# Projecting the context's keys and values for two batches at once, in a kernel of four transformer layers

## The chip, the cores and the metric

The kernel runs on one core of a Trainium2 chip, as one program. The metric is device time in microseconds (us), from launch to end. TensorE has two clock levels, 1.2 and 2.4 GHz; the profile gives the clock that was granted as a share of the higher one.

## The reference

The input x is 8 batches of 512 tokens of width 256; each batch has a context of 64 rows of width 192. Four layers follow, each on the layer-normed x, each added to x: cross attention (8 heads of 64) on the context; a 16-expert network of which each token uses 4; a second, top-32 cross attention on the same context (4 heads of 32) whose result sets scale and shift around a long convolution, with an MLP behind it; and an 8-expert layer in which each expert picks its 512 best tokens. What the change touches is the start of both attentions:

```
k = (context @ W_k).reshape(b, j, HEADS, DIM_HEAD)      # 64 rows, 512 columns for each batch
v = (context @ W_v).reshape(b, j, HEADS, DIM_HEAD)
...
K = (x_vision @ Wk).reshape(Bb, Gg, H, DH)              # 64 rows, 128 columns
V = x_vision @ Wv                                       # 64 rows, 256 columns
```

## The kernel before

The first three layers run as a software pipeline over the 8 batches in `layers_block`. A hand-written list, `SCHEDULE`, gives every engine the same order of steps (stage, batch, name, part); each engine takes from it the steps it has a function for, waits on semaphores inside them, and never reorders. Stages of three neighbouring batches overlap: ATTEND of batch b+2, MID of batch b+1 and LAST of batch b. A fourth family of steps, KERN, builds the convolution's kernel in the first 240 us. `experts_block` follows with the last layer: it gathers 512 token rows for each of 8 experts with indirect DMAs issued on GpSimd (POOL, line 2087), multiplies, and adds the rows back with others (line 2097), four of each for an expert.

Everything is in float32, and each float32 matmul appears in the trace as two matmul instructions, each with its own weight load. The step `keys` part 0 projects the context in `ctx_first` (96 partitions, two halves of the width): K into PSUM bank KT, V into bank VT, 16 instructions each with the weights stationary and 64 context columns moving. ScalarE (ACT, lines 1500 and 1501) then copies each bank into `ktbd` and `vtbd`, whose off-diagonal blocks GpSimd has zeroed once at the start (line 793). Part 1 multiplies `ktbd` by the query weights (M, into `m0`), part 2 multiplies `vtbd` by the output weights (VO). `attend` makes the scores S from `m0`; VectorE (DVE) takes their maximum (line 1125), ScalarE the exponential, GpSimd scales them (line 859), and TensorE turns the result (PT, line 1681). The step `text` part 0 does the same for the second attention from `ctx_second`: 12 instructions into bank KV1, then copies into `k1bd` and `v1T`. In the order of the list, odd and even batches have the same steps at nearly the same places: `keys` 0 stands just behind `mlp_out` and beside `back`, whose second half (the FO pair for tiles 2 and 3, lines 1891 and 1895) can only start when VectorE has emptied the banks of tiles 0 and 1 in `film_out` (line 1343).

The SP queue loads the contexts, one batch at a time, some batches ahead (`load_ahead`, `load_second`). The first DVE step of KERN waits until GpSimd has made all its constants (`blanks_made`, 20).

Of the kernel before, what the change touches and what calls it, by code (L numbers as in the profile page):

```python
# [23 lines left out]
P = 128  # L24
B, T, D = 8, 512, 256
NT = T // P
DC = D // P
# [417 lines left out]
def layers_block(nc, ctx, S, A, out):  # L445
    with ExitStack() as tmp:
# [45 lines left out]
        lower_half, upper_half = slice(0, J), slice(J, 2 * J)  # L492
        v1T = sb("v1T", [P, DC, J])
        m1 = sb("m1", [P, DC, H1 * J])
# [130 lines left out]
        def _(sp):  # L625
# [5 lines left out]
            def load_ahead(b):  # L631
                sp.wait_ge(*at(b - 1, "filled", "VT"))
                apart(sp)
                sp.dma_start(ctx0[:], ctx_h[b]).then_inc(*tick("ctx0_loaded"))

# [5 lines left out]
            def load_second(b):  # L641
                sp.wait_ge(*at(b - 1, "filled", "KV1"))
                apart(sp)
                sp.dma_start(ctx1[:], ctx_h[b]).then_inc(*tick("ctx1_loaded"))

# [44 lines left out]
            sp.dma_start(ctx0[:], ctx_h[0]).then_inc(*tick("ctx0_loaded"))  # L690
            load("wk", kv_in)
# [16 lines left out]
            load("values", values_in)  # L708
            sp.dma_start(ctx1[:], ctx_h[0]).then_inc(*tick("ctx1_loaded"))
            for name in ("wk1", "wv1", "b_out", "route"):  # L710
# [718 lines left out]
        def _(a):  # L1429
# [122 lines left out]
            def text(b, part):  # L1552
                if part == 0:
                    a.wait_ge(*at(b, "filled", "KV1"))
                    for h in range(H1):
                        lanes = slice(h * DH1, (h + 1) * DH1)
                        nc.scalar.copy(k1bd[lanes, h * J:(h + 1) * J], bank("KV1")[lanes, 0:J])
                    nc.scalar.copy(v1T[:], bank("KV1")[:, J:3 * J].rearrange("p (k j) -> p k j", k=DC)).then_inc(*tick("emptied", "KV1"))
                if part == 1:
# [110 lines left out]
        def _(pe):  # L1670
# [80 lines left out]
            def keys(b, part):  # L1751
                if part == 0:
                    if first(b):
                        pe.wait_ge(kv_in, 32)
                    pe.wait_ge(*at(b, "ctx0_loaded"))
                    for use, w in (("KT", S["wk"]), ("VT", S["wv"])):
                        o = bank(use)
                        product(b, use, parts=[p for c in range(C0) for p in contract(
                            o[:, c * J:(c + 1) * J], [(w[:, k, c * P:(c + 1) * P], ctx0[:, k, :]) for k in range(2)])])
                if part == 1:  # L1760
                    if first(b):
                        pe.wait_ge(wq_centred, 1)
                    pe.wait_ge(*at(b, "emptied", "KT"))
                    for k in range(DC):
                        product(b, "M", k, parts=[p for c in range(C0) for p in contract(
                            bank("M", k)[:, c * P:(c + 1) * P], [(S["wqT"][:, c, k * P:(k + 1) * P], ktbd[:, c, :])])])
                if part == 2:
                    if first(b):
                        pe.wait_ge(wo_in, 32)
                    pe.wait_ge(*at(b, "emptied", "VT"))  # L1770
                    for k in range(2):
                        product(b, "VO", k, parts=[p for c in range(2) for p in contract(
                            bank("VO", k)[:, c * D:(c + 1) * D], [(vtbd[:, 2 * k + c, :], S["wo"][:, 2 * k + c, :])])])

# [77 lines left out]
            def text(b, part):  # L1852
                if part == 0:
                    if first(b):
                        pe.wait_ge(text_in, 64)
                    pe.wait_ge(*at(b, "ctx1_loaded"))
                    o = bank("KV1")
                    product(b, "KV1", parts=contract(o[:, 0:J], [(S["wk1"][:, k, :], ctx1[:, k, :]) for k in range(2)])
                            + [p for c in range(DC) for p in contract(
                                o[:, (c + 1) * J:(c + 2) * J], [(S["wv1"][:, k, c * P:(c + 1) * P], ctx1[:, k, :]) for k in range(2)])])  # L1860
                if part == 1:
                    pe.wait_ge(*at(b, "emptied", "KV1"))
                    product(b, "MM1", parts=[p for k in range(DC) for p in contract(
                        bank("MM1")[:, k * D:(k + 1) * D], [(S["wq1T"][:, k * P:(k + 1) * P], k1bd[:])])])
                if part == 2:
                    if first(b):
                        pe.wait_ge(film_folded, 3)
                    pe.wait_ge(*open_(b, "VF"))
                    for c in range(DC):
                        low_ = nc.tensor.matmul(bank("VF")[lower_half, :], v1T[:, c, :], S["wfilm"][:, c, 0:512], start=(c == 0), stop=(c == DC - 1))  # L1870
                        if c == DC - 1:
                            low_.then_inc(*tick("film_low"))
                        high_ = nc.tensor.matmul(bank("VF")[upper_half, :], v1T[:, c, :], S["wfilm"][:, c, 512:1024], start=(c == 0), stop=(c == DC - 1))
                    high_.then_inc(*tick("filled", "VF"))
# [433 lines left out]
def build(nc, A, out):  # L2308

    with ExitStack() as ctx:  # L2310
# [11 lines left out]
        with ExitStack() as weights:  # L2322
# [26 lines left out]
            wb("xT", [P, DC, T])  # L2349
            wb("ctx_first", [CK, 2, J])  # L2350
            wb("ctx_second", [CK, 2, J])
            wb("mgate", [P, 1])
# [64 lines left out]
```

## Time and profile before

| | |
|---|---|
| median of 3 runs | 1424.18 us (1421.99 to 1427.73) |
| the profiled execution | 1421.83 us, of it 1420.0 us from the first to the last instruction |
| mean granted TensorE clock | 0.924 |
| TensorE busy (matmul) | 1231.5 us (87%), 5325 instructions |
| VectorE busy | 922.0 us (65%) |
| ScalarE busy | 479.5 us (34%) |
| GpSimd busy | 340.1 us (24%) |
| layers | 0 to 1152 us |
| experts | 1152 to 1420 us |

A row of the timeline is: start, duration from the first to the last of merged instructions, engine, line, operation, output and inputs, shape and count, and in brackets how long the engine was idle before and for whom. A share of busy time is a mean over stages with different limits, so the stages have to be read one by one.

### The profile page before, as it was taken

What the parts mean: (1) busy time and instruction counts of PE and PEld (TensorE: products, weight loads), DVE (VectorE), ACT (ScalarE), POOL (GpSimd) and SP (SyncE); (2) the same over time, 40 slices, a digit from 0 to 9 for tenths busy, and PEclk for the clock granted to TensorE, in tenths of its full rate; (3) what the DMA queues carried; (4) which work ended last, traced back from release to release, by engine and by line L of the source; (5) the groups of instructions that cost most, each with busy time, mean ns of one, the idle gap of its engine ahead of it and who ended that gap; (6) DMA issues with size and microseconds to landing.
All of it is one profiled execution on the core that took longest, in us unless ns stands there. A gap on an engine that the chain in (4) does not pass through costs nothing. (4 is left out here: it accounts for less than half of the span.)

```text
span 1420.0 us, 17680 instructions
## 1 busy us (share of the span) xinstructions
PE 1231.5 (87%) x5325; PEld 743.2 (52%) x5325; DVE 922.0 (65%) x3415; ACT 479.5 (34%) x860; POOL 340.1 (24%) x603
## 2 busy tenths in 40 slices
PE   5776967998999899799989979999687439999996
PEld 3543544555466465455546635554364326667764
DVE  6767897778768767777867877797974581111110
ACT  3534431163153326215332531532412422322221
POOL 4223220033023112202212220320203222322331
PEclk9787978999999999999989999999898659999999
DMA  9002003000300300210030030021000135433421
GB/s 289 25 15 61 19 1 76 18 1 17 90 19 1 106 18 1 61 46 18 15 91 18 1 97 25 3 61 38 1 0 1 61 111 165 143 90 90 96 37 18
DMA packets 45353, 72.54 MB, mean 51 GB/s; under 512 B 8549, under 2 KB 27208, under 8 KB 45130
## 3 DMA queue, kind: packets, MB, share of 16 engines
q1 hardware_dynamic: 39114, 62.88, 15.0%
q0 software_dynamic: 6144, 8.52, 3.4%
q8 instruction: 43, 0.70, 0.2%
q14 instruction: 52, 0.43, 0.1%
HBM read 58.27 MB, written 13.07 MB: 50 GB/s over the span
## 5 line engine op out<-in xcount | busy, mean ns | idle before, releaser
L835 POOL TENSOR_SCALAR ve<-mv 128x2 f32<-128x2 f32 x74 | 16.9, 228 | 515.2 <-DVE mv L1103 515.1
L1675 PE MATMUL ps<-x,keys 128*128 128x512 f32 x256 | 124.4, 610 | 1.8 <-DVE hT L1197 1.8
L1840 PE MATMUL ps<-hT,values 128*128 128x512 f32 x256 | 120.0, 598 | 0.0
L2290 PE MATMUL experts_ps<-experts_yT,experts_fc 128*128 128x512 f32 x256 | 113.4, 601 | 1.2 <-ACT experts_yT L2215 1.2
L2302 PE MATMUL experts_ps<-experts_fc,experts_hT 128*128 128x256 f32 x512 | 112.0, 379 | 0.8 <-ACT experts_hT L2227 0.8
L1675 PE MATMUL ps<-zT_second,w 128*128 128x512 f32 x224 | 104.5, 606 | 6.2 <-ACT big L1616 3.9
L2302 PEld LDWEIGHTS experts_ps<-experts_fc,experts_hT 128*128 128x128 f32 x512 | 96.7, 190 | 14.5 <-ACT experts_hT L2227 1.6
L1675 PE MATMUL ps<-w,big 128*128 128x256 f32 x448 | 99.0, 379 | 0.8 <-ACT big L1616 0.8
L2199 DVE SCALAR_TENSOR_TENSOR experts_o<-experts_ps,experts_wh,experts_b2w 128x256 f32<-128x256 f32 x32 | 15.5, 484 | 128.7 <-PE experts_ps L2302 128.7
L2227 ACT ACTIVATE experts_hT<-experts_ps,experts_b 128x512 f32<-128x512 f32 x64 | 44.0, 687 | 156.9 <-PE experts_ps L2290 156.9
L1675 PEld LDWEIGHTS ps<-w,big 128*128 128x128 f32 x448 | 84.1, 190 | 12.5 <-ACT big L1616 1.6
L2097 POOL DMA_INDIRECT out_x<-experts_o,experts_idx x32 | 51.8, 1618 | 156.1 <-DVE experts_o L2199 154.2
L1840 PEld LDWEIGHTS ps<-hT,values 128*128 128x128 f32 x256 | 49.1, 192 | 61.2 <-issue 61.0
L2290 PEld LDWEIGHTS experts_ps<-experts_yT,experts_fc 128*128 128x128 f32 x256 | 48.7, 193 | 60.0 <-issue 59.9
L1675 PEld LDWEIGHTS ps<-x,keys 128*128 128x128 f32 x256 | 47.9, 195 | 56.5 <-issue 50.6
L1235 DVE MATCH_REPLACE8 work<-rest,work 128x64 f32<-128x64 f32 x384 | 76.2, 210 | 0.4
L1675 PEld LDWEIGHTS ps<-zT_second,w 128*128 128x128 f32 x224 | 40.9, 193 | 51.7 <-issue 39.5
L1675 PE MATMUL ps<-m,xT 128*128 128x512 f32 x128 | 64.9, 631 | 0.0
L859 POOL TENSOR_TENSOR e_buf<-e_buf,rs 128x512 f32<-128x512 f32 x32 | 33.3, 1042 | 120.8 <-DVE rs L1122 120.8
L1675 PE MATMUL ps<-hT,vo 128*128 128x512 f32 x128 | 59.2, 617 | 0.7 <-ACT hT L1486 0.7
L1231 DVE MAX8 rest<-work 128x8 f32<-128x64 f32 x384 | 57.5, 212 | 0.0
L841 POOL TENSOR_TENSOR rstd<-ve,power 128x2 f32<-128x2 f32 x74 | 54.3, 734 | 6.2
(445 smaller groups left out, 2448.1 us busy)
## 6 DMA issues: line engine op xcount, KB each, us to landing
gT<-expert_gates SPq DMA_DIRECT2D x32, 512.0 KB, 7.9
experts_fc<-in_fc1T SPq DMA_DIRECT2D x8, 1024.0 KB, 5.1
experts_fc<-in_fc2T SPq DMA_DIRECT2D x8, 1024.0 KB, 8.6
xT<-in_xT SPq DMA_DIRECT2D x8, 512.0 KB, 3.6
x<-in_x SPq DMA_DIRECT2D x8, 512.0 KB, 3.5
expert_table<-tb SPq DMA_DIRECT2D x7, 528.0 KB, 9.9
out_x<-x SPq DMA_DIRECT2D x7, 512.0 KB, 9.2
w<-in_W SPq DMA_DIRECT2D x2, 1024.0 KB, 9.5
```

Of the source, the lines that this page charges most:

```text
L835: nc.gpsimd.tensor_scalar(o, i, c, None, ALU.add).then_inc(*tick(*event))
L841: nc.gpsimd.tensor_tensor(o, i, power[:].unsqueeze(1).to_broadcast(i.shape), ALU.pow).then_inc(*tick(*event))
L859: nc.gpsimd.tensor_tensor(probs, probs, rs[:, t, :].unsqueeze(2).to_broadcast([P, H0, J]), ALU.mult).then_inc(*tick("pr", t))
L1231: nc.vector.max(best[:, h, :], src[:, h, :]).then_inc(*tick("tm8", t, n, h))
L1235: nc.vector.match_replace(work[:, t, h, :], best[:, h, :], src[:, h, :], OUT_OF_RANGE).then_inc(*tick("tmr", t, n, h))
L1675: last = nc.tensor.matmul(o, l, r_, start=start, stop=stop)
L1840: last = nc.tensor.matmul(bank("O2", k), S["values"][:, c, k * P:(k + 1) * P], hT[:, c % RING, :], start=(c == 0), stop=(c == HC - 1))
L2097: g.indirect_dma_start(out_rows, bass.IndirectOffsetOnAxis(ap=idx[:, e, c:c + 1], axis=0), o[e % 2][:, c, :], None, compute_op=ALU.add).th ...
L2199: nc.vector.scalar_tensor_tensor(o[s][:, c, :], o_bank(CC * e + c), wh[s][:, c:c + 1], b2w[s][:, c, :], ALU.mult, ALU.add).then_inc(out_ma ...
L2227: nc.scalar.activation(hT[e % 2][:, m, :], g_bank(m), ACT.Gelu_apprx_tanh, bias=b1[:, e, m:m + 1]).then_inc(hidden_made, 1)
L2290: last = nc.tensor.matmul(g_bank(m), fc1[e % 3][:, k, m * P:(m + 1) * P], yT[e % 2][:, k, :], start=(k == 0), stop=(k == DC - 1))
L2302: last = nc.tensor.matmul(o_bank(at), hT[e % 2][:, m, c * P:(c + 1) * P], fc2[e % 3][:, m, :], start=(m == 0), stop=(m == HC - 1))
```

## The change

At an even batch, the contexts of batches b and b+1 lie side by side in doubled tiles, and each projection moves 128 columns in place of 64 into the same PSUM bank. The copies fill both halves of doubled `ktbd`, `vtbd`, `k1bd` and `v1T`. At an odd batch TensorE and ScalarE only wait and count the semaphores on, and the later products read the half `b % 2`. The SP queue loads two contexts at even batches and none at odd ones; at batch 0 it issues one more load of each kind. The tiles grow by 6.5 KB in each partition; the reserved room for descriptors of dynamic (GpSimd-issued) DMAs shrinks from the default 16384 bytes to 8192.

```diff
             def load_ahead(b):
-                sp.wait_ge(*at(b - 1, "filled", "VT"))
+                if b % 2:
+                    return
+                sp.wait_ge(*at(b - 2, "filled", "VT"))
                 apart(sp)
-                sp.dma_start(ctx0[:], ctx_h[b]).then_inc(*tick("ctx0_loaded"))
+                for of in range(2):
+                    sp.dma_start(ctx0[:, :, of, :], ctx_h[b + of]).then_inc(*tick("ctx0_loaded"))
...
                     for use, dst in (("KT", ktbd), ("VT", vtbd)):
                         a.wait_ge(*at(b, "filled", use))
-                        src = bank(use)[:, 0:C0 * J].rearrange("p (c j) -> p c j", c=C0)
-                        nc.scalar.copy(dst[0:64, :, 0:J], src[0:64])
-                        nc.scalar.copy(dst[64:P, :, J:2 * J], src[64:P]).then_inc(*tick("emptied", use))
+                        if b % 2:
+                            apart(a)
+                            a.sem_inc(*tick("emptied", use))
+                            continue
+                        src = bank(use).rearrange("p (c of j) -> p of c j", c=C0, of=2)
+                        nc.scalar.copy(dst[0:64, :, :, 0:J], src[0:64])
+                        nc.scalar.copy(dst[64:P, :, :, J:2 * J], src[64:P]).then_inc(*tick("emptied", use))
...
-                    pe.wait_ge(*at(b, "ctx0_loaded"))
+                    if b % 2 == 0:
+                        pe.wait_ge(*at(b + 1, "ctx0_loaded"))
                     for use, w in (("KT", S["wk"]), ("VT", S["wv"])):
+                        if b % 2:
+                            pe.wait_ge(*open_(b, use))
+                            apart(pe)
+                            pe.sem_inc(*tick("filled", use))
+                            continue
                         o = bank(use)
                         product(b, use, parts=[p for c in range(C0) for p in contract(
-                            o[:, c * J:(c + 1) * J], [(w[:, k, c * P:(c + 1) * P], ctx0[:, k, :]) for k in range(2)])])
+                            o[:, c * P:(c + 1) * P], [(w[:, k, c * P:(c + 1) * P], ctx0[:, k, :, :].rearrange("p of j -> p (of j)")) for k in range(2)])])
...
-            wb("ktbd", [P, C0, P])
-            wb("vtbd", [P, C0, P])
-            wb("k1bd", [P, H1 * J])
+            wb("ktbd", [P, 2, C0, P])
+            wb("vtbd", [P, 2, C0, P])
+            wb("k1bd", [P, 2, H1 * J])
...
-    nc = bacc.Bacc("TRN2", target_bir_lowering=False, num_devices=1)
+    nc = bacc.Bacc("TRN2", target_bir_lowering=False, num_devices=1, dynamic_dma_scratch_size=8192)
```

The step `text` part 0 is changed in the same way (bank KV1, tiles `ctx_second`, `k1bd`, `v1T`).

## Rows read from the trace of the kernel before

**Rows 1.** Windows: busy us of each engine (instructions), granted clock, DMA share, GB/s.

```profile
150.00:250.00 100.00, 78.72 (x478) 50.98 (x477) 85.50 (x325) 34.52 (x59) 15.75 (x28) 0.86 0.14 34
850.00:950.00 100.00, 98.45 (x377) 56.67 (x375) 79.05 (x344) 31.82 (x57) 17.96 (x34) 0.98 0.11 31
```

**Rows 2.** Timeline of TensorE: K, V, FO pair and M of batch 4.

```profile
516.23 1.90 PE L1675 MATMUL ps<-ctx_first,wk 96*128 96x64 f32 x16
517.96 1.95 PE L1675 MATMUL ps<-ctx_first,wv 96*128 96x64 f32 x16
519.85 0.39 PE L1891 MATMUL ps<-film_bias,ones_bf 64*128 64x512 bf16 x2
521.02 2.05 PE L1675 MATMUL ps<-ktbd,wqT 128*128 128x128 f32 x16
522.91 1.89 PE L1675 MATMUL ps<-wo,vtbd 128*128 128x256 f32 x8
```

**Rows 3.** Timeline of TensorE: KV1 of batch 1, and what follows it.

```profile
246.94 0.56 PE L1675 MATMUL ps<-ctx_second,wk 96*128 96x64 f32 x4
...
248.23 1.94 PE L1675 MATMUL ps<-x,keys 128*128 128x512 f32 x4
```

**Rows 4.** Timeline, batch 1: VectorE's waits for TensorE behind `keys`.

```profile
167.88 0.63 DVE L1231 MAX8 top<-ps 128x8 f32<-128x64 f32 x4 [0.38 <-PE ps L1675]
172.54 0.69 DVE L1125 TENSOR_REDUCE mx<-ps 128x8 f32<-128x512 f32 x1 [0.61 <-PE ps L1675]
176.50 0.69 DVE L1125 TENSOR_REDUCE mx<-ps 128x8 f32<-128x512 f32 x1 [0.39 <-PE ps L1675]
```

**Rows 5.** Timeline, batch 7: from `keys` to the first turned probabilities.

```profile
877.76 2.00 PE L1675 MATMUL ps<-ctx_first,wk 96*128 96x64 f32 x16
...
879.57 0.42 DVE L1343 TENSOR_TENSOR xf<-xf,ps 128x256 f32<-128x256 f32 x1
...
881.57 0.61 PE L1891 MATMUL ps<-film_bias,ones_bf 64*128 64x512 bf16 x2
...
883.91 0.42 DVE L1341 TENSOR_TENSOR xf<-yv,ps 128x256 f32<-128x256 f32 x1 [0.88 <-PE ps L1895]
...
889.84 0.69 DVE L1125 TENSOR_REDUCE mx<-ps 128x8 f32<-128x512 f32 x1 [1.31 <-PE ps L1675]
...
893.05 1.04 POOL L859 TENSOR_TENSOR e_buf<-e_buf,rs 128x512 f32<-128x512 f32 x1 [3.31 <-DVE rs L1122]
...
894.46 0.60 PE L1681 MATMUL ps<-ident,e_buf 128*128 128x128 f32 x4
```

**Rows 6.** Timeline, batch 5: the same chain behind `keys`.

```profile
655.81 0.69 DVE L1125 TENSOR_REDUCE mx<-ps 128x8 f32<-128x512 f32 x1 [2.04 <-PE ps L1675]
...
659.42 1.04 POOL L859 TENSOR_TENSOR e_buf<-e_buf,rs 128x512 f32<-128x512 f32 x1 [10.06 <-DVE rs L1122]
...
661.29 0.60 PE L1681 MATMUL ps<-ident,e_buf 128*128 128x128 f32 x4
```

**Rows 7.** Timeline of TensorE: the wait behind KV1 of batch 7.

```profile
977.64 1.98 PE L1675 MATMUL ps<-x,keys 128*128 128x512 f32 x4 [0.34 <-DVE hT L1197]
```

**Rows 8.** Windows just behind `keys` of batches 2 and 7.

```profile
281.00:285.00 4.00, 4.00 (x19) 2.41 (x18) 2.99 (x12) 1.00 (x3) 1.88 (x4) 0.63 0.12 27
881.60:885.50 3.90, 3.90 (x18) 2.31 (x18) 2.82 (x11) 0.80 (x3) 1.86 (x4) 0.60 0.00 0
```

**Rows 9.** Timeline of the start: one zeroed tile, and VectorE's first instruction.

```profile
3.62 0.53 POOL L793 MEMSET ktbd<- 128x512 f32 x1
...
7.33 0.89 DVE L951 TENSOR_TENSOR zT_second<-big 128x256 f32<-128x256 f32 x2 [7.33 <-POOL work L798]
```

**Rows 10.** The page: one group of costs, and DMA issues with median us to landing.

```profile
L2097 POOL DMA_INDIRECT out_x<-experts_o,experts_idx x32 | 51.8, 1618 | 156.1 <-DVE experts_o L2199 154.2
...
experts_rows<-expert_table,experts_idx POOLq DMA_INDIRECT x32, 4.1
out_x<-experts_o,experts_idx POOLq DMA_INDIRECT x32, 3.8
```

More of the change, by code:

```diff
@@ L492, in layers_block @@
         lower_half, upper_half = slice(0, J), slice(J, 2 * J)
-        v1T = sb("v1T", [P, DC, J])
+        v1T = sb("v1T", [P, 2, DC, J])
         m1 = sb("m1", [P, DC, H1 * J])
@@ L641, in load_second @@
             def load_second(b):
-                sp.wait_ge(*at(b - 1, "filled", "KV1"))
+                if b % 2:
+                    return
+                sp.wait_ge(*at(b - 2, "filled", "KV1"))
                 apart(sp)
-                sp.dma_start(ctx1[:], ctx_h[b]).then_inc(*tick("ctx1_loaded"))
+                for of in range(2):
+                    sp.dma_start(ctx1[:, :, of, :], ctx_h[b + of]).then_inc(*tick("ctx1_loaded"))
             def spread_gates(b):
@@ L689, in _ @@
                     sp.dma_start(dst[rows_, :], src).then_inc(par_in, 16)
-            sp.dma_start(ctx0[:], ctx_h[0]).then_inc(*tick("ctx0_loaded"))
+            for of in range(2):
+                sp.dma_start(ctx0[:, :, of, :], ctx_h[of]).then_inc(*tick("ctx0_loaded"))
             load("wk", kv_in)
@@ L708, in _ @@
             load("values", values_in)
-            sp.dma_start(ctx1[:], ctx_h[0]).then_inc(*tick("ctx1_loaded"))
+            for of in range(2):
+                sp.dma_start(ctx1[:, :, of, :], ctx_h[of]).then_inc(*tick("ctx1_loaded"))
             for name in ("wk1", "wv1", "b_out", "route"):
@@ L1554, in text @@
                     a.wait_ge(*at(b, "filled", "KV1"))
+                    if b % 2:
+                        apart(a)
+                        a.sem_inc(*tick("emptied", "KV1"))
+                        return
                     for h in range(H1):
                         lanes = slice(h * DH1, (h + 1) * DH1)
-                        nc.scalar.copy(k1bd[lanes, h * J:(h + 1) * J], bank("KV1")[lanes, 0:J])
-                    nc.scalar.copy(v1T[:], bank("KV1")[:, J:3 * J].rearrange("p (k j) -> p k j", k=DC)).then_inc(*tick("emptied", "KV1"))
+                        nc.scalar.copy(k1bd[lanes, :, h * J:(h + 1) * J], bank("KV1")[lanes, 0:2 * J].rearrange("p (of j) -> p of j", of=2))
+                    nc.scalar.copy(v1T[:], bank("KV1")[:, 2 * J:6 * J].rearrange("p (k of j) -> p of k j", k=DC, of=2)).then_inc(*tick("emptied", "KV1"))
                 if part == 1:
@@ L1765, in keys @@
                         product(b, "M", k, parts=[p for c in range(C0) for p in contract(
-                            bank("M", k)[:, c * P:(c + 1) * P], [(S["wqT"][:, c, k * P:(k + 1) * P], ktbd[:, c, :])])])
+                            bank("M", k)[:, c * P:(c + 1) * P], [(S["wqT"][:, c, k * P:(k + 1) * P], ktbd[:, b % 2, c, :])])])
                 if part == 2:
@@ L1772, in keys @@
                         product(b, "VO", k, parts=[p for c in range(2) for p in contract(
-                            bank("VO", k)[:, c * D:(c + 1) * D], [(vtbd[:, 2 * k + c, :], S["wo"][:, 2 * k + c, :])])])
+                            bank("VO", k)[:, c * D:(c + 1) * D], [(vtbd[:, b % 2, 2 * k + c, :], S["wo"][:, 2 * k + c, :])])])
             def attend(b, s):
@@ L1855, in text @@
                         pe.wait_ge(text_in, 64)
-                    pe.wait_ge(*at(b, "ctx1_loaded"))
+                    if b % 2:
+                        pe.wait_ge(*open_(b, "KV1"))
+                        apart(pe)
+                        pe.sem_inc(*tick("filled", "KV1"))
+                        return
+                    pe.wait_ge(*at(b + 1, "ctx1_loaded"))
                     o = bank("KV1")
-                    product(b, "KV1", parts=contract(o[:, 0:J], [(S["wk1"][:, k, :], ctx1[:, k, :]) for k in range(2)])
+                    both = [ctx1[:, k, :, :].rearrange("p of j -> p (of j)") for k in range(2)]
+                    product(b, "KV1", parts=contract(o[:, 0:P], [(S["wk1"][:, k, :], both[k]) for k in range(2)])
                             + [p for c in range(DC) for p in contract(
-                                o[:, (c + 1) * J:(c + 2) * J], [(S["wv1"][:, k, c * P:(c + 1) * P], ctx1[:, k, :]) for k in range(2)])])
+                                o[:, (c + 1) * P:(c + 2) * P], [(S["wv1"][:, k, c * P:(c + 1) * P], both[k]) for k in range(2)])])
                 if part == 1:
@@ L1863, in text @@
                     product(b, "MM1", parts=[p for k in range(DC) for p in contract(
-                        bank("MM1")[:, k * D:(k + 1) * D], [(S["wq1T"][:, k * P:(k + 1) * P], k1bd[:])])])
+                        bank("MM1")[:, k * D:(k + 1) * D], [(S["wq1T"][:, k * P:(k + 1) * P], k1bd[:, b % 2, :])])])
                 if part == 2:
@@ L1869, in text @@
                     for c in range(DC):
-                        low_ = nc.tensor.matmul(bank("VF")[lower_half, :], v1T[:, c, :], S["wfilm"][:, c, 0:512], start=(c == 0), stop=(c == DC - 1))
+                        low_ = nc.tensor.matmul(bank("VF")[lower_half, :], v1T[:, b % 2, c, :], S["wfilm"][:, c, 0:512], start=(c == 0), stop=(c == DC - 1))
                         if c == DC - 1:
                             low_.then_inc(*tick("film_low"))
-                        high_ = nc.tensor.matmul(bank("VF")[upper_half, :], v1T[:, c, :], S["wfilm"][:, c, 512:1024], start=(c == 0), stop=(c == DC - 1))
+                        high_ = nc.tensor.matmul(bank("VF")[upper_half, :], v1T[:, b % 2, c, :], S["wfilm"][:, c, 512:1024], start=(c == 0), stop=(c == DC - 1))
                     high_.then_inc(*tick("filled", "VF"))
@@ L2349, in build @@
             wb("xT", [P, DC, T])
-            wb("ctx_first", [CK, 2, J])
-            wb("ctx_second", [CK, 2, J])
+            wb("ctx_first", [CK, 2, 2, J])
+            wb("ctx_second", [CK, 2, 2, J])
             wb("mgate", [P, 1])
```

1 line of the change is left out of this document (added).

## The prediction

> **What bounds the kernel now.** I read the page first, then windows of 100 us, then the timeline around each place that the change touches, TensorE and VectorE side by side. The page's chain covers only the experts' stage, which the change leaves alone, so the layers had to be read by stages. In the steady layers TensorE is the limit: 98.45 of 100 us busy, VectorE 79.05 [rows 1]. Before 250 us it is the other way round, VectorE 85.5 and TensorE 78.7 [rows 1], because it builds the convolution's kernel. Since every engine keeps its written order, the question for each removed group is: how far can VectorE follow before TensorE has to wait for it?
>
> **What is removed.** Four `keys` groups (batches 1, 3, 5, 7) and four KV1 groups. From start to start, 16 K instructions take 517.96 - 516.23 = 1.73 us and 16 V instructions 519.85 - 517.96 = 1.89, so a `keys` group is 3.6 us [rows 2]. KV1 is 248.23 - 246.94 = 1.3 us [rows 3]. All eight together are 4 x 3.6 + 4 x 1.3 = 19.6 us of TensorE, the most that the removal alone could give. ScalarE's copies of odd batches go too, but nothing in the steady part waits for them, so they count nothing; if ScalarE were late, M would wait, and it stands idle for over 1 us before each.
>
> **What the wider groups cost.** M, also 16 instructions but with 128 moving columns, takes 522.91 - 521.02 = 1.89 us [rows 2], as much as V with 64. So a matmul here costs about 0.11 us with either width, and the width is hidden under something that both share. The bounds are nothing (V's price) and 1.89 - 1.73 = 0.16 for every 16 instructions (K's price), which over 44 instructions in the three later even batches is 1.3 us. I take 0.3, since V is the nearer row for half of them.
> The Trainium skill (TensorE: Matmul & The Clock Gate, Back-to-back issue gap) has a table in which up to 64 columns cost some 60 cycles and 128 columns 134; by that rule alone the wider matmul would cost about twice the narrow one, nothing would be saved, and the result would be some 1.5 us slower than before. The trace disagrees: 0.108 us for 64 columns and 0.118 for 128.
>
> **Batch 1.** VectorE is the limit here. Behind the group it waits for TensorE 0.38, 0.61 and 0.39 us [rows 4], and then works through until past the next stalls of TensorE. So 1.4 of the 3.6 us come through, and the rest turns into a longer wait of TensorE for the probabilities.
>
> **Batches 3 and 7.** Directly behind the group stands the second FO pair, which needs what VectorE empties at 879.57 + 0.42 = 879.99. Now it starts at 881.57 [rows 5]. Without the 3.6 us TensorE arrives near 878 and waits some 2 us, so 881.57 - 879.99 = 1.6 us come through. The next check is the turned probabilities at 894.46: VectorE can gain its waits of 0.88 + 1.31 = 2.2, and GpSimd ended at 893.05 + 1.04 = 894.09, 0.4 before TensorE needed it [rows 5], so up to 2.5 may pass and 1.6 does. Batch 3 has the same order and the same 1.6. Together 3.2.
>
> **Batch 5.** Here both FO pairs stand ahead of the group. VectorE gains its wait of 2.04 and a smaller one of 0.59 before it; GpSimd ended at 660.46 and TensorE turned at 661.29 [rows 6], so at most 2.6 + 0.8 = 3.4 passes: I take 3.4 of 3.6.
>
> **KV1.** Batches 1, 3 and 5 stand in stretches where VectorE next waits for TensorE by several us, and TensorE for nobody: 3 x 1.3 = 3.9. Behind KV1 of batch 7 TensorE already waits 0.34 us for VectorE, which is at work without a gap [rows 7]; nothing comes through, and the wait grows to 1.6.
>
> **The clock.** Right behind the `keys` groups of batches 2 and 7 the granted clock is 0.63 and 0.60 [rows 8], with TensorE busy all the time: so about 3 of 4 us run at 1.2 GHz in place of 2.4 and half of that, 1.5 us, is lost. It was the same behind 3 and 5, and not behind 1, 4 and 6. What ran just before each fall was 32 matmuls of 64 columns, with no wait. After the change no such group is left. If the falls go, batch 2 gives 1.4; in 3 and 7 the limit of 2.5 from the probabilities leaves 0.9 each, and in batch 5 nothing is left to take. That is 3.2 at most, nothing at least (a fall may have another cause, or a new one may come with the new waits of 2 us in batches 3 and 7). I take 1.5.
>
> **The start.** GpSimd zeroes twice as much before it releases VectorE, whose first instruction at 7.33 waited for exactly that [rows 9]. At 0.53 us for 512 elements, 1280 more cost 1.3 us; with a fixed part in each instruction less. I take 1.2, all of it on the path, as the chain from there to TensorE's first taps and on to 240 us is VectorE's. Between nothing and 1.3. The two extra context loads in the SP queue (some 0.5 us of issue each) delay the weights' loads, but TensorE's first projections end long before it stands waiting for VectorE, so they cost nothing; without that cover, 0.5. In the even batches ScalarE's copies double in length; M follows V and the FO pair, which hide them. In the steady part the SP queue loses waits for TensorE and gains none; the contexts are there over 100 us early.
>
> **Descriptor room.** Only the 64 indirect DMAs use it, in the experts' stage. GpSimd spends 1.6 us on each and stands idle 156 us before the scatters [rows 10]. I take nothing.
>
> **The sum.** 1.4 + 3.2 + 3.4 + 3.9 + 1.5 - 0.3 - 1.2 = 11.9 us. The profiled execution took 1421.83 us, 1.8 around its span of 1420.0; it would take 1409.9. The median of the runs is 1424.18, 2.4 above the profiled one, so on its scale I forecast 1412. With the bounds of width, start and clock the forecast's own range is 1408 to 1416.
>
> **Rivals.**
> *VectorE takes it back.* The waits that VectorE can give up in the odd batches are small, and if the picks of the top-32 land ahead of the softmax in its order, the `keys` groups of batches 3, 5 and 7 give nothing: 11.9 - 3.2 - 3.4 - 1.5 = 3.8 us are left, 1420. For it: batch 1 shows just that. Against it: rows 5 and 6 leave room by the row. Chance 0.17.
> *All of it comes through.* Later waits shrink as well, and 19.6 - 1.5 = 18.1 us are won: 1406; with the clock 1404. For it: VectorE waits for TensorE often in each batch. Against: the FO pair in 3 and 7, VectorE's stretch in batch 1. Chance 0.12.
> *The new waits bring the clock down.* Two waits of 2 us in batches 3 and 7, and falls at other places; at 1.5 us a fall, as in rows 8, four more falls cost 6: 1418. Chance 0.10.
> *The smaller descriptor room makes GpSimd wait: slower.* If each indirect DMA had to wait for the one before to land, it would cost 4.1 and 3.8 us in place of 1.6 [rows 10]. Four gathers before the first expert cost 10 more, four scatters behind the last 9 more; in between 253 us of transfers fit in the stage's 268. 1412 + 19 = 1431 or a little above, slower than before. It decides from 1.5 us more for each of these eight. Against it: the transfers of one expert are few and those of the one before have been waited for. Chance 0.05. The Trainium skill (DMA: Bandwidth & Descriptors, SWDGE vs HWDGE vs iDMA) says that GpSimd appends such descriptors to rings in SBUF, which is how a smaller room could be felt; no row here shows a full one.
> That the change does not do what it says (widths not merged) has 0.01; the forecast has 0.55.
>
> **How the numbers follow.** Half a per cent, 7.1 us, is about what a measurement of this kernel can tell from no change: the line is 1417. Faster: the forecast nearly whole (0.54), the second rival (0.12), and the edges of the first and third (0.04): 0.70. Slower: the fourth, and 0.01 for the unforeseen: 0.06. The rest, 0.24, is within half a per cent. The range of 8 in 10 reaches up into the first rival and down to the second: 1404 to 1421.
>
> **What would show it.** TensorE's instructions fall by 4 x 44 = 176; K with 128 columns still starts V within 1.73 to 1.9 us; VectorE's first instruction comes at 8.4 to 8.6; TensorE waits some 2 us for line 1343 in batches 3 and 7, and 1.6 in place of 0.34 behind the first products of the last MID stage; the clock stays at 1.0 behind the even groups; the experts' stage keeps its 268 us. The prediction is wrong if the batches' distances shrink at places without removed work, or if the shift that each group gives is found again as a longer wait of TensorE for the probabilities.

## The result, and the profile after

The changed kernel takes 1404.67 us in the median of 4 runs (1403.3 to 1405.65) against 1425.15 of 4 runs of the kernel before: a ratio of 0.9857, 95% interval 0.9833 to 0.988, so 20.5 us faster. In 4 later runs of the same kernel it was 1405.37 against 1422.05, or 16.7 us faster, ratio 0.9879 (0.9863 to 0.9896). The forecast was 1412, or 12 us faster. The direction is right, and the gain was under-sized: the time lies near the lower end of the stated range (1404 to 1421) and below the forecast's own range of 1408 to 1416. Times here and below are medians of fast runs; one run of `wide_all` below, 1447.01 us at a granted clock of 0.887, was slow and is left out.

The profiled execution took 1405.65 us. The page's first part, of the kernel after (engine, busy us, share, instructions):

```profile
span 1403.8 us, 17324 instructions
...
PE 1206.8 (86%) x5149; PEld 718.5 (51%) x5149; DVE 920.2 (66%) x3415; ACT 474.2 (34%) x824; POOL 341.8 (24%) x603
```

TensorE has 176 instructions less, as counted. Its busy time fell by 24.7 us where the removed groups were 19.6. The clock would account for the other 5: by the mean granted clocks of 0.924 and 0.927, 1420.0 x 0.076 = 107.9 us were lost to it before and 1403.8 x 0.073 = 102.5 after (an estimate from the two pages).

The two traces were laid side by side, instruction by instruction, as every engine keeps its order. The table gives one VectorE or GpSimd instruction for each stretch, its start before and after, and how much earlier it comes. "Step" is the difference from the line above; the forecast is the prediction's term for that stretch, without its clock term of 1.5, which was given for batches 2, 3 and 7 together. A "fall" is a stretch in which the clock goes from 2.4 to 1.2 GHz and comes back some us later.

| start before | after | earlier by | step | what lies in the stretch | forecast |
|---|---|---|---|---|---|
| 159.39 | 160.28 | -0.89 | -0.89 | start, wider groups of batch 0 | -1.2 |
| 199.89 | 200.06 | -0.17 | +0.72 | `keys`, batch 1 | 1.4 |
| 277.61 | 276.55 | 1.06 | +1.23 | KV1, batch 1 | 1.3 |
| 300.34 | 297.76 | 2.58 | +1.52 | wide `keys`, batch 2: clock alone | clock |
| 380.16 | 379.18 | 0.98 | -1.60 | nothing changed here: a fall of the clock | 0 |
| 419.75 | 415.80 | 3.95 | +2.97 | `keys`, batch 3, and a fall gone | 1.6 and clock |
| 485.53 | 482.32 | 3.21 | -0.74 | nothing changed here: a fall | 0 |
| 529.73 | 525.23 | 4.50 | +1.29 | KV1, batch 3; wide `keys`, batch 4 | 1.3 |
| 615.23 | 612.09 | 3.14 | -1.36 | nothing changed here: falls | 0 |
| 679.48 | 670.74 | 8.74 | +5.60 | `keys`, batch 5, and a fall of 7 us gone | 3.4 and clock |
| 739.92 | 727.95 | 11.97 | +3.23 | KV1, batch 5, inside a fall that is 7 us shorter | 1.3 |
| 830.93 | 819.01 | 11.92 | -0.05 | wide `keys`, batch 6 | width |
| 857.98 | 844.58 | 13.40 | +1.48 | nothing changed here: a fall gone | 0 |
| 900.15 | 885.41 | 14.74 | +1.34 | `keys`, batch 7 | 1.6 and clock |
| 990.05 | 975.33 | 14.72 | -0.02 | KV1, batch 7 | 0 |
| 1050.07 | 1038.54 | 11.53 | -3.19 | nothing changed here: falls | 0 |
| 1299.29 | 1286.14 | 13.15 | +1.62 | end of the layers: shorter falls | 0 |

At the end of GpSimd's last scatter the difference is still 13.14 us, but the span is 16.2 us shorter. The missing 3.1 lie behind that scatter (below, room_only). The other 4.3 of the 20.5 are between profile and median: before, the profiled execution is 3.3 faster than the median of 1425.15, after, it is 1.0 slower.

### The profile page after: what moved, and what is told of

Read it like the earlier page. It is cut to its first block and busy times, and to the rows that moved or that the text cites. A ratio compares the mean times of both kernels' runs of the same rounds, so it can differ in the third digit from the quotient of the medians.

```text
span 1403.8 us, 17324 instructions
## 1 busy us (share of the span) xinstructions
PE 1206.8 (86%) x5149; PEld 718.5 (51%) x5149; DVE 920.2 (66%) x3415; ACT 474.2 (34%) x824; POOL 341.8 (24%) x603
## 3 DMA queue, kind: packets, MB, share of 16 engines
q0 software_dynamic: 6144, 8.52, 3.4%
```

## The steps, each with its rows

**Start.** Timeline of VectorE, after. Its first instruction was forecast at 8.4 to 8.6, waiting for GpSimd; compare [rows 9]:

```profile
8.40 0.88 DVE L959 TENSOR_TENSOR zT_second<-big 128x256 f32<-128x256 f32 x2 [8.40 <-POOL work L806]
```

**Width.** Timeline of TensorE, after, batch 4, beside [rows 2]:

```profile
511.68 1.95 PE L1691 MATMUL ps<-ctx_first,wk 96*128 96x128 f32 x16
513.47 1.95 PE L1691 MATMUL ps<-ctx_first,wv 96*128 96x128 f32 x16
515.35 0.39 PE L1919 MATMUL ps<-film_bias,ones_bf 64*128 64x512 bf16 x2
```

K takes 1.79 us with 128 columns (1.73 with 64), V 1.88 (1.89): 0.05 for the group. The batch-6 line of the table says the same. A matmul takes 0.11 us at either width. The Trainium skill (TensorE: Matmul & The Clock Gate, LDWEIGHTS) puts a weight load, in ns, at its columns divided by 1.2: an estimate of 107 ns for 128, in which the moving columns do not enter. The rows agree with that: 1.73 / 16 = 0.108 us with 64 moving columns and 1.79 / 16 = 0.112 with 128. That the load sets the pace at either width is a reading; no run changes the columns of the weights.

**Batch 1.** Timeline of TensorE, after, at the turned probabilities:

```profile
177.05 0.65 PE L1697 MATMUL ps<-ident,e_buf 128*128 128x128 f32 x4 [2.89 <-POOL e_buf L867]
177.64 0.38 PE L1691 MATMUL ps<-mask_rows,ones_bf 1*128 1x512 bf16 x1
177.95 3.28 PE L1691 MATMUL ps<-m,xT 128*128 128x512 f32 x4
181.64 0.77 PE L1697 MATMUL ps<-ident,e_buf 128*128 128x128 f32 x4 [0.41 <-POOL e_buf L867]
```

Before, this wait was 0.82: the freed time became a longer wait, as forecast. Right behind it the four score matmuls took 3.28 us, where they had taken 1.98: the clock fell behind the longer wait, VectorE had to wait for the scores, and half of the 1.4 was lost again. Two later kernels in which no fall stands at that spot, `narrow_half` and `late_6k`, have 1.66 and 1.65 there.

**Batches 3 and 7.** Timeline of TensorE, after, the second FO pair of either batch:

```profile
396.56 0.39 PE L1919 MATMUL ps<-film_bias,ones_bf 64*128 64x512 bf16 x1 [0.97 <-DVE xf L1351]
397.81 0.39 PE L1919 MATMUL ps<-film_bias,ones_bf 64*128 64x512 bf16 x1 [0.86 <-DVE xf L1351]
...
865.40 0.39 PE L1919 MATMUL ps<-film_bias,ones_bf 64*128 64x512 bf16 x1 [0.96 <-DVE xf L1351]
866.64 0.39 PE L1919 MATMUL ps<-film_bias,ones_bf 64*128 64x512 bf16 x1 [0.86 <-DVE xf L1351]
```

1.83 and 1.82 us of new waits for VectorE's line 1351 (1343 before), where some 2 were forecast.

**Batch 5, and what VectorE lets through.** Timeline of TensorE, after; the same check as the last row of [rows 6]:

```profile
652.48 0.66 PE L1697 MATMUL ps<-ident,e_buf 128*128 128x128 f32 x4 [0.82 <-POOL e_buf L867]
```

GpSimd does set it now, with a wait of 0.82, but at 652.48 in place of 661.29: 8.8 earlier, of which 3.1 had been won before the batch. VectorE's waits for TensorE between the group and this check, in the kernel before, were these (the last one is in [rows 6], 2.04):

```profile
647.71 0.63 DVE L1231 MAX8 top<-ps 128x8 f32<-128x64 f32 x4 [2.03 <-PE ps L1675]
651.04 0.63 DVE L1231 MAX8 top<-ps 128x8 f32<-128x64 f32 x4 [0.59 <-PE ps L1675]
```

After, all three are 0. The prediction counted the second and the third, 2.6 us, and not the first. With it the limit is 2.03 + 0.59 + 2.04 + 0.8 = 5.5 us, and 5.60 came. For batch 3 the prediction took over the limit of batch 7. Its own waits, before, were longer, and both are 0 after:

```profile
402.58 0.42 DVE L1341 TENSOR_TENSOR xf<-yv,ps 128x256 f32<-128x256 f32 x1 [1.49 <-PE ps L1895]
408.54 0.63 DVE L1231 MAX8 top<-ps 128x8 f32<-128x64 f32 x4 [1.25 <-PE ps L1675]
```

With a third of 0.17 they make 2.9, and 2.97 came. In batch 7 the wait of 0.88 went, but that of 1.31 only shrank to 0.92, so 1.3 came.

**KV1 of batch 7.** Timeline of TensorE, after; 0.34 in [rows 7], 1.6 forecast:

```profile
962.91 1.98 PE L1691 MATMUL ps<-x,keys 128*128 128x512 f32 x4 [1.44 <-DVE hT L1205]
```

**The clock.** Windows, after (us; busy us of PE, PEld, DVE, ACT, POOL with instructions; granted clock, DMA share, GB/s): behind the groups' places of batches 2, 3, 5 and 7, and then four other places:

```profile
280.20:284.20 4.00, 4.00 (x26) 2.65 (x22) 3.37 (x13) 2.33 (x5) 1.88 (x4) 1.00 0.01 2
398.00:402.00 4.00, 4.00 (x26) 2.93 (x24) 3.76 (x14) 1.26 (x3) 2.14 (x4) 1.00 0.03 6
633.00:641.00 8.00, 8.00 (x32) 4.26 (x31) 6.85 (x20) 0.27 (x1) 1.17 (x3) 1.00 0.26 78
868.00:872.00 4.00, 4.00 (x22) 4.00 (x23) 3.74 (x14) 1.09 (x2) 1.87 (x4) 0.57 0.00 0
359.00:363.00 4.00, 3.46 (x9) 2.80 (x10) 1.51 (x4) 0.59 (x1) 0.00 (x0) 0.57 1.07 223
588.00:602.00 14.00, 10.16 (x27) 5.53 (x26) 6.55 (x14) 2.28 (x5) 0.00 (x0) 0.51 0.76 180
711.00:718.00 7.00, 4.30 (x12) 3.03 (x13) 2.89 (x8) 4.02 (x7) 0.00 (x0) 0.51 1.08 227
824.00:828.00 4.00, 3.58 (x13) 1.48 (x11) 3.83 (x11) 3.97 (x9) 0.00 (x0) 1.00 0.16 52
```

The same places in the kernel before (the place of 359 lies at 365 there, 588 at 598, 711 at 717, 824 at 833):

```profile
365.00:369.00 4.00, 4.00 (x13) 2.05 (x12) 2.81 (x6) 0.00 (x0) 0.00 (x0) 1.00 1.02 329
598.00:605.00 7.00, 5.71 (x16) 3.83 (x13) 2.23 (x5) 1.17 (x2) 0.00 (x0) 0.51 1.04 220
717.00:732.00 15.00, 12.34 (x40) 8.99 (x41) 3.91 (x11) 7.51 (x17) 0.00 (x0) 0.54 0.83 213
833.00:837.00 4.00, 3.28 (x11) 1.45 (x12) 3.62 (x13) 0.64 (x2) 0.00 (x0) 0.57 0.01 2
```

The falls behind batches 2, 3 and 5 are gone; behind batch 7 one remains, now behind the new waits. Others changed at places that the change does not touch: new at 359, longer at 588 (14 us against 7), shorter at 711 (7 against 14), gone at 824. Between 250 and 1100 us, TensorE had just been idle for 1.8 us or more ahead of each of these others, eight before and nine after; ahead of the four behind the narrow `keys` groups it had not been idle at all. Idle time alone does not tell where a fall comes: each of the two traces also has about six stretches with as much of it and no fall behind.

## The experiments

**The descriptor room.** `room_only` is the kernel before with one edit, `room_12k` the same with a value between:

```diff
-    nc = bacc.Bacc("TRN2", target_bir_lowering=False, num_devices=1)
+    nc = bacc.Bacc("TRN2", target_bir_lowering=False, num_devices=1, dynamic_dma_scratch_size=8192)
```

> The kernel before with the smaller room for descriptors (8192 bytes) and nothing else. In the two traces GpSimd's last scatter ends 13.1 us earlier after the change, but the span ends 16.2 us earlier: behind that scatter 7.9 us pass before and 4.9 after. Theory A: the room sets that tail (and perhaps more outside the profile), and this kernel is 3 us faster than before, with a tail near 4.9 us. Theory B: the tail differs from execution to execution, the room is worth nothing, and the time is that of before within 1 us. The rival of the forecast, GpSimd waiting for room, would show as scatters or gathers over 1.6 us and a slower time.

> The kernel before with a room of 12288 bytes, between its default of 16384 and the 8192 of the change. From GpSimd's last scatter to the end of the span 7.9 us passed with 16384 and 4.9, 4.9, 5.1 and 4.9 in the four traces with 8192. Theory A, the tail grows with the room: 6.4 us here. Theory B, the tail is 4.9 or 7.9 by something else than size (a threshold, chance): one of these two.

room_only: 1421.2 us (12 runs) against 1423.58 (19 runs), ratio 0.9984 (0.9967 to 1.0002). By times alone that could be nothing. The traces decide. Here are GpSimd's last scatter, from the timeline, and the span, from the view of cores, for the kernel before (16384 bytes):

```profile
1410.51 1.55 POOL L2097 DMA_INDIRECT out_x<-experts_o,experts_idx  x1 [1.90 <-DVE experts_o L2199]
```

```profile
core 0: 1420.0 us, clock 0.924
```

for room_12k (12288):

```profile
1411.12 1.55 POOL L2097 DMA_INDIRECT out_x<-experts_o,experts_idx  x1 [1.90 <-DVE experts_o L2199]
```

```profile
core 0: 1419.1 us, clock 0.925
```

and for the changed kernel (8192):

```profile
1397.37 1.55 POOL L2125 DMA_INDIRECT out_x<-experts_o,experts_idx  x1 [1.90 <-DVE experts_o L2227]
```

```profile
core 0: 1403.8 us, clock 0.927
```

The tails are 1420.0 - 1412.06 = 7.94, 1419.1 - 1412.67 = 6.43 and 1403.8 - 1398.92 = 4.88 us; room_only itself has 1419.7 - 1414.80 = 4.90. Theory A holds with its number. Up to here the tail costs 0.37 us for 1024 bytes; it is 3.1 us of the change's gain. The view of the last source line says which instruction it is: GpSimd's DRAIN (each engine runs one at the program's end, and GpSimd's ends last), behind the landing of the last scatter (3.8 and 3.7 us after its issue, before and after). In this order, for the kernel before, room_12k, the changed kernel and late_6k (6144 bytes, below):

```profile
L2003 POOLq DRAIN  x1: 5297/5297/5297, 1414.5 to 1414.5; - x1
L2003 POOLq DRAIN  x1: 3787/3787/3787, 1415.1 to 1415.1; - x1
L2031 POOLq DRAIN  x1: 2276/2276/2276, 1401.3 to 1401.3; - x1
L2031 POOLq DRAIN  x1: 2276/2276/2276, 1398.2 to 1398.2; - x1
```

These are ns. It takes 5297 in narrow_half too, which has the default room, and 2276 in every trace with 8192. That GpSimd would wait for room during the experts (the slower rival) is refuted: a scatter takes 1.62 us and a gather 1.00 with 16384, 12288 and 8192 bytes alike. `room_12k` was run once, 1420.93 against 1422.05; it rests on its trace.

Behind 170 us room_only's trace stays 2.6 to 2.8 us behind that of before, in all but 2% of the instructions: the falls of the clock repeat with the work. The one difference is from 140 to 165 us, where room_only has a granted clock of 0.89 from 138 to 170 and before 1.00; that made room_only's engines 2.7 late in this one execution. One of its two falls there begins in the last us of the narrow `keys` group of batch 1, behind which none stands before. For these two executions the whole difference is thus made ahead of 170 us; where that of the other runs is made, no trace shows.

**Width without removal.** `wide_all` is the changed kernel with the projections kept at odd batches (the results are rewritten and not copied), KV1's too; shown is the first attention's part:

```diff
                     for use, w in (("KT", S["wk"]), ("VT", S["wv"])):
-                        if b % 2:
-                            pe.wait_ge(*open_(b, use))
-                            apart(pe)
-                            pe.sem_inc(*tick("filled", use))
-                            continue
```

> The changed kernel with the projections kept at the odd batches too (128 columns, both contexts, the same values written again and not copied), so that TensorE removes nothing and only the width differs from before. Theory A, narrow matmuls bring the clock down: the falls behind the keys groups of batches 2, 3, 5 and 7 are gone although all groups stand, and the layers end some 4 us earlier than before. Theory B, the falls behind the groups have another cause and their places shift with anything: as many falls as before, the layers end 1 to 2 us later than before (start 1, width up to 1.3). The changed kernel lost 16 stretches of granted clock between 250 and 1100 us, as many as before, at other places.

wide_all takes 1417.01 us (7 runs) against 1423.58, ratio 0.9951 (0.993 to 0.9973): 6.6 us faster with not one TensorE instruction less (5325). The profiled executions differ by 4.4, and 3 of that are the room. In the trace the steps against before are +1.5 over batch 2, +1.5 over 3, +3.0 over 5 and +1.5 over 7, 7.5 together, and -0.05 over batches 4 and 6, which had no fall to lose. The rest of the course gives back most of it: -2.1 by 200 us (start, width and falls there), -0.9, -0.6 and -1.4 near 365, 475 and 600 us, +1.7 near 725, -1.1 near 850 and -1.5 behind 1000, so that 1.4 are left at the last experts. Windows of wide_all behind the four groups:

```profile
280.00:290.00 10.00, 10.00 (x62) 7.11 (x62) 8.53 (x28) 4.11 (x7) 3.03 (x7) 1.00 0.21 62
402.00:410.00 8.00, 8.00 (x43) 5.36 (x42) 6.45 (x31) 3.61 (x7) 4.67 (x9) 1.00 0.06 14
644.00:654.00 10.00, 10.00 (x57) 7.27 (x56) 8.90 (x64) 3.98 (x8) 6.20 (x10) 1.00 0.05 11
882.00:890.00 8.00, 8.00 (x43) 5.88 (x43) 6.23 (x18) 4.20 (x11) 2.79 (x7) 1.00 0.00 0
```

**Removal without width.** `narrow_half` is the kernel before with the odd batches' projections and copies left out (they use the keys and values of the batch before), in TensorE and ScalarE, for both attentions; shown is TensorE's part of the first:

```diff
                     for use, w in (("KT", S["wk"]), ("VT", S["wv"])):
+                        if b % 2:
+                            pe.wait_ge(*open_(b, use))
+                            apart(pe)
+                            pe.sem_inc(*tick("filled", use))
+                            continue
```

> The kernel before, 64 columns and default room, with the projections and copies of the odd batches left out: an odd batch then uses the keys and values of the batch before it. So it removes the same 176 instructions and widens nothing. Theory A, two separate gains (a narrow group brings the clock down behind it; removed work comes through where VectorE allows): the fall behind the group of batch 2 near 280 us is there, as before, and none stands behind the places of batches 3 and 5; no 1.07 us is lost at the start. Against the changed kernel's trace the lag is about +1 until 280, 0 to -0.5 behind it, and the tail 3 us longer: a span some 4 us above the changed kernel's 1403.8, 1408, and a time of 1409 to 1411. Theory B, the falls follow TensorE's whole course and not the narrow groups: no fall near 280, or other falls behind 3 and 5, and a time under 1407.

1411.29 us (6 runs) against 1422.2, ratio 0.993 (0.9909 to 0.995), and a span of 1407.1: theory A. Timeline of narrow_half at batch 2, and under it the windows behind the groups of batches 2 and 6:

```profile
273.80 2.00 PE L1683 MATMUL ps<-ctx_first,wk 96*128 96x64 f32 x16
275.63 1.95 PE L1683 MATMUL ps<-ctx_first,wv 96*128 96x64 f32 x16
277.52 0.48 PE L1909 MATMUL ps<-film_bias,ones_bf 64*128 64x512 bf16 x2
277.79 1.92 PE L1913 MATMUL ps<-vf,amT 64*128 64x512 f32 x4
```

```profile
277.00:282.00 5.00, 5.00 (x27) 3.36 (x26) 4.04 (x14) 1.22 (x3) 1.88 (x4) 0.66 0.09 21
748.00:753.00 5.00, 5.00 (x27) 3.29 (x26) 3.22 (x13) 1.89 (x4) 1.85 (x4) 0.66 0.10 25
```

Behind the narrow group of batch 2 the clock falls in the middle of unbroken work, and here behind that of batch 6 too, which it had not before; there the fall cost 1.6 us. Behind the places of batches 3 and 5 it does not fall. The step over batch 5 is 5.6 as in the changed kernel, that over batch 3 3.0, that over 7 1.4, and KV1 gives 2.2 in batch 1 and 3.1 in batch 5. Its tail is 1407.1 - 1399.17 = 7.93: the default room again.

Counted over all traces, leaving out batch 0: with 64 columns a fall begins within 1 us of the end of a `keys` group in 15 of 24 places (before 4 of 7, room_only 5 of 7, room_12k 4 of 7, narrow_half 2 of 3), with 128 columns in 0 of 25 (eighteen places in the six kernels and executions that merge the projections, seven in wide_all). The late start is no rival for that: in late_blanks and late_6k below VectorE starts earlier than before, and they have none either. What spares batch 4, where no narrow group is followed by a fall in any trace, is open.

**Keys alone.** `keys_only` leaves `text`, `ctx_second`, `k1bd` and `v1T` as before.

> The change for the first attention alone; the second one's contexts stay one batch at a time. Two traces side by side put the KV1 groups' removal at 1.3 (b1), 1.35 (b3), 3.2 (b5, with two falls of the clock less) and 0 (b7). Theory A, parts add up by their places: this kernel stands 4 us (3 x 1.3) above the changed one, 1409, and 16 below before. Theory B, what the keys groups freed is only kept because KV1 is gone too, or falls of the clock land otherwise: over 3 us from 1409 either way.

1408.52 us against 1423.58, ratio 0.9893 (0.987 to 0.9917): theory A by its number, and its last scatter comes 3.0 us later than the changed kernel's. KV1's share is 3 to 4 us. Place by place it is less tidy: the KV1 groups are worth 1.3, 1.3, 2.0 and 0 in batches 1, 3, 5 and 7, or 4.7, and falls at untouched places, of which keys_only has fewer, give back the rest. Of the 3.2 at KV1 of batch 5, keys_only has 1.2 without touching that group.

**The same again.** `after_again` is the changed kernel, unaltered.

> The changed kernel once more, unaltered. Its four times were 1403.3 to 1405.65 on one chip, while the kernel before spread over 1418 to 1428 in 19 runs. If falls of the clock repeat with the work, its trace has lags of under 1 us against the first one behind 250 us, falls near 359, 465, 588 to 602 and 711 us, and none behind the places of batches 2, 3 and 5. If they are chance, the falls are elsewhere. Median 1403 to 1408.

1405.37 us (4 runs). The falls stand within 1 us of the first trace's, and from 180 us to the end the two differ by under 0.3 us in all but 1% of VectorE's and GpSimd's instructions. The falls at untouched places are therefore not chance from one execution to the next; they belong to this kernel's course, as the ones behind narrow groups belonged to the one before.

**The new waits filled.** `m_between` moves M of batches 3 and 7, with the step of the second attention beside it, ahead of the second FO pair in the order of all engines (batch 7 shown):

```diff
-    (LAST, 5, "film_out", 2), (LAST, 5, "back", 3),
-    (ATTEND, 7, "keys", 1), (MID, 6, "text", 0),
+    (LAST, 5, "film_out", 2),
+    (ATTEND, 7, "keys", 1), (MID, 6, "text", 0), (LAST, 5, "back", 3),
```

> The changed kernel with M (and in batch 3 the second attention's product) of batches 3 and 7 ahead of the second FO pair, in every engine's order. TensorE waits there 0.97 + 0.86 and 0.96 + 0.86 us for line 1351 in the changed kernel. Theory A: these waits vanish, the product fills them, and up to 1.8 us in each of the two batches come through, less what the turned probabilities then wait for VectorE (0.9 each at least): 2 to 3.5 faster. Theory B: VectorE's second half of film_out comes later by the 1.9 us of M, and with it the next stage: nothing won, or up to 2 us lost. In batch 7 the clock's fall at 868 us, behind the wait, should go with the wait under theory A.

1409.63 us, ratio 0.9904 (0.9887 to 0.9922): 4.3 slower than after_again beside it. The waits for line 1351 are gone, and others stand a few us on; the timeline of m_between in batch 3, and under it a window behind these waits:

```profile
410.64 0.66 PE L1697 MATMUL ps<-ident,tb 128*128 128x128 f32 x4 [0.83 <-ACT tb L1623]
411.68 0.66 PE L1697 MATMUL ps<-ident,tb 128*128 128x128 f32 x4 [0.39 <-ACT tb L1623]
```

```profile
412.00:417.00 5.00, 5.00 (x12) 2.07 (x10) 3.52 (x27) 0.68 (x2) 1.16 (x1) 0.66 0.02 3
```

Behind them the clock falls, and batch 3 loses 1.5 us, batch 7 3.4 (there behind a wait of 2.55 for the turned probabilities, and at a clock of 0.54 from 883 to 894 us). So theory B, with the clock on top. In this trace 5 us more were lost from 50 to 65 us, at a granted clock of 0.68 from 45 to 70 against 0.86; that is in the stretch where executions scatter, and no part of the verdict on the edit.

**Zeroing off the path, and a smaller room still.** `late_blanks` zeroes the doubled tiles behind GpSimd's last constant; `late_6k` has a room of 6144 bytes besides:

```diff
-            for name in ("ktbd", "vtbd", "k1bd"):
-                blank(g.memset(S[name][:], 0.0))
...
             g.tensor_tensor(cen[:, 0, :], cen[:, 1, :], ident[:], ALU.add).then_inc(blanks_made, 1)
+            for name in ("ktbd", "vtbd", "k1bd"):
+                g.memset(S[name][:], 0.0).then_inc(blanks_made, 1)
```

> The changed kernel with the zeroing of the three doubled tiles moved behind GpSimd's last constant, so that VectorE's first instruction doesn't wait for it. Three memsets of some 1.07, 1.07 and 0.3 us leave the path: VectorE starts at about 6.0 in place of 8.40. Theory A, VectorE's chain sets the first 240 us: 2.4 us faster there, about 2 at the end. Theory B, the loads of weights set the pace at 19 to 28 us and again near 90 us, where the changed kernel's lag of 1.07 had shrunk to 0.62: under 1 us comes through, or falls of the clock swallow it.

> The changed kernel with late zeroing, and a room of 6144 bytes. The tail was 7.94 us with 16384 bytes, 6.43 with 12288 and 4.9 to 5.1 with 8192: 0.37 us for 1024 bytes. Theory A, this line goes on and GpSimd still never waits for room: the tail is 4.2, indirect DMAs take 1.6 us each as before, and the kernel is 0.7 faster than late zeroing alone (1403.9), ratio to before about 0.986. Theory B, room runs out for a transfer: indirect DMAs over 1.6 us, and a time above 1404. The line may also have a floor at 4.9.

Timeline of VectorE's first instruction in late_blanks:

```profile
5.98 0.88 DVE L959 TENSOR_TENSOR zT_second<-big 128x256 f32<-128x256 f32 x2 [5.98 <-ACT big L1441]
```

It starts 2.4 us earlier, yet from 40 to 80 us nothing is left of that (-0.1), then it is 0.8 at 100 us, 0.5 late at 240, 0.5 early at 260 and 1.7 early at the end, against the first trace of the changed kernel. The time is 1403.9, ratio 0.9871 (0.9854 to 0.9887), 1.5 below after_again, with intervals that overlap: theory B for the start itself; the later gains come at falls. late_6k takes 1402.61, ratio 0.9867 (0.9847 to 0.9887), the lowest median of all, but not told apart from late_blanks. Its last scatter and span:

```profile
1394.27 1.55 POOL L2125 DMA_INDIRECT out_x<-experts_o,experts_idx  x1 [2.03 <-DVE experts_o L2227]
```

```profile
core 0: 1400.7 us, clock 0.926
```

A tail of 1400.7 - 1395.82 = 4.88, and the same DRAIN of 2276 ns: the line does not go on below 8192, and 6144 bytes neither help nor make GpSimd wait.

## Why the prediction was right, and where it was not

**Right, by its own steps.** The sizes of the removed groups and their count; the width's price (0.3 forecast, 0.05 for a group measured), against the rule that would have doubled it; VectorE's start at 8.40; the new waits for line 1351 in batches 3 and 7; the wait of 1.44 behind KV1 of batch 7 and its gain of nothing; the 1.3 of KV1 in batches 1 and 3; the wait for the probabilities that took batch 1's time; that GpSimd does not wait for room. (Its 1.6 us hold for the scatters, which [rows 10] shows; the gathers take 1.00.) The first rival, VectorE taking it back, did not come: batches 3 and 5 gave 8.6 together.

**The terms that were mis-sized: what VectorE lets through, and with it the clock.** The clock was put at 1.5 us, 3.2 at most, because VectorE was held to limit what a faster TensorE could pass on: 0.9 more in batches 3 and 7, nothing in batch 5. That limit was wrong in two places. In batch 5 a wait of 2.03 us was left out, so that 5.5 could pass and not 3.4, and the fall there is 7 us long, twice the others. In batch 3 the limit was taken from batch 7, where it is smaller. The removed group (3.6) and the fall (half of 7) offer 7.1 us in batch 5, and VectorE lets 5.6 through; how much of that is clock and how much is removal has no single answer. Width alone is worth 3.0 there (wide_all), width and removal together 5.60, and removal without width, in a kernel that has no fall there, 5.6 too.

That the 64-column groups bring on the falls behind them is shown: with 128 columns they go though the work stays (wide_all, 7.5 us together), with 64 columns the fall of batch 2 stays though other work goes (narrow_half), and the count is 15 of 24 against 0 of 25.

Beyond the removal's terms, the changed kernel gained 1.5 in batch 2, 2.97 - 1.6 = 1.4 in batch 3 and 5.60 - 3.4 = 2.2 in batch 5: 5.1 at the `keys` groups. Another 3.23 - 1.3 = 1.9 came at KV1 of batch 5, in a fall that before begins at 717 us, 6 us ahead of that group; it is no fall behind narrow work. Against these 7.0 stand -1.60, -0.74, -1.36, +1.48, -3.19 and +1.62 at places that the change leaves alone, -3.8 together, which the prediction had at nothing. Net, 3.2 us in place of 1.5. So it is partly luck that the sum for the engines came out only 1.2 off: of the 7.0 won, 3.8 was lost again at other places, and batches 1 and 7 gave 0.9 less than forecast.

The prediction named as a sign of being wrong that the distances shrink at places without removed work. By +1.48 near 840 us and +1.62 at the end of the layers they do, and elsewhere they grow. What sets the falls at these places is open: they come behind waits of TensorE, repeat from run to run, and move when the course changes a few us ahead of them. The Trainium skill (TensorE: Matmul & The Clock Gate, Part 1) says that a slow clock is the default and that activity releases it. The falls behind waits agree; the falls amid unbroken narrow matmuls (4.00 of 4 us busy at 0.63, [rows 8]) do not, if what the profile counts as busy is that activity.

**The term that was missing: the end.** "I take nothing" for the descriptor room looked for a price in the 64 indirect DMAs alone, and bounded it upwards only. The room costs at the end of the program, in GpSimd's DRAIN behind the last scatter: 3.0 of the 3.1 us by which the tail is shorter.

**The scale.** 1412 was made for a kernel before of 1424.18. For the profiled execution the sum gave 1409.9 and 1405.65 came: 4.3 off, of which the tail is 3.1 and the engines 13.1 - 11.9 = 1.2. The other 3 of the 7.3 between forecast and median come from the scale: the median after lies 1.0 below its profiled execution, where 2.4 above it was assumed (3.4, less 0.3 of rounding). The second rival has the measured number (1404 to 1406) for another reason: not all of the removed time came through (nothing at KV1 of batch 7, 1.34 of 3.6 in batch 7, 0.72 of 3.6 in batch 1).

## What to carry to other kernels

A group of many narrow matmuls can cost twice: its own time, which here was the same at twice the width, and the clock in the work behind it (15 of 24 places here); so look at the granted clock behind such a group before pricing its removal or its merging, and expect the falls elsewhere to move. When pricing what one engine lets through, add up every wait from the change to the next check, in each batch by itself. When a setting reserves memory, look behind the last work too, and bound its effect on both sides. Compare traces by how much earlier the same instruction comes: the table above places each gain and loss to within a few us, where times of whole runs scatter by 9 us (1418.14 to 1427.62 for the kernel before).

## What the runs showed of the hardware that was not expected

The falls of TensorE's clock are no noise in this kernel: in two executions of the changed kernel they stand within 1 us of each other behind 180 us. In the traces of before and after, between 250 and 1100 us, they begin either just behind idle time of TensorE (1.8 us or more) or at the end of 32 unbroken matmuls with 64 moving columns; behind such matmuls with 128 columns none began in any trace. The time between the last scatter and the end of the span was 7.94 and 7.93 us with 16384 bytes reserved for descriptors, 6.43 with 12288, 4.9 to 5.1 in seven traces with 8192, and 4.88 with 6144; what changes in it is GpSimd's DRAIN of 5.30, 3.79, 2.28 and 2.28 us.
